# A decoder layer on one core: the four-bit quantisation of the normalised row split over two chunks of the cross-attention

## The reference, cut to what matters

```python
def fp4_quant_dequant(x):
    xb = x.reshape(shape[:-1] + (shape[-1] // BLOCK, BLOCK))      # BLOCK = 16
    scale = jnp.max(jnp.abs(xb), axis=-1, keepdims=True) / 6.0
    scale = jnp.maximum(scale, jnp.float32(1e-12))
    xn = xb / scale
    idx = jnp.searchsorted(_MID, jnp.abs(xn))
    q = _GRID[idx] * jnp.sign(xn) * scale
...
# cross-attention: q = ln(x) @ W.T + b
logits = jnp.einsum('bqd,bmd->bqm', q, memories) + add_mask
out = jnp.einsum('bqm,bmd->bqd', jax.nn.softmax(logits, axis=-1), memories)
# feed-forward
gate = fp4_linear(x, w_gate)
y = fp4_linear(x, w_up)
h = jax.nn.silu(gate) * y
return fp4_linear(h, w_down)
...
x = x + _L0_attn_ref(_layernorm(x), ...)
x = x + _L0_xattn_ref(_layernorm(x), ...)
x = x + _L0_ffn_ref(_layernorm(x), ...)
```

## Time and profile before

| what | us |
|---|---|
| median of 3 runs (lowest, highest) | 549.69 (549.15, 549.93) |
| the profiled execution | 550.32 |
| its span | 548.6 |
| around the span | 1.7 |
| TensorE busy in the span | 497.0 (91%) |
| VectorE busy | 360.2 (66%) |
| ScalarE busy | 335.9 (61%) |
| GpSimd busy | 170.9 (31%) |

### The profile page before, as it was taken

How to read it: one execution, slowest core, us unless ns; L and a number is a source line. 1 busy time by engine, 2 the same in 40 slices (tenths; PEclk the granted TensorE clock), 3 DMA queues, 4 the chain that set the end, 5 groups by cost and what they waited for, 6 DMA issues and landing times.

```text
span 548.6 us, 9765 instructions
## 1 busy us (share of the span) xinstructions
PE 497.0 (91%) x3480; PEld 324.7 (59%) x3480; DVE 360.2 (66%) x858; ACT 335.9 (61%) x659; POOL 170.9 (31%) x292
## 2 busy tenths in 40 slices
PE   7359899999999999988979989989898998989997
PEld 6206333333333333324548979979797897878896
DVE  6899988878887778813554365647666466664345
ACT  4626777787877787886663746637274472637520
POOL 6820124544444443335434231322223112210000
PEclk9857999999999999999998999989999898999999
DMA  8985300042006100030597324343243433400000
GB/s 241 289 263 119 89 1 2 4 119 57 1 3 142 35 1 4 1 118 8 161 295 219 116 87 135 87 125 109 77 116 91 117 92 82 140 25 1 6 6 6
DMA packets 27956, 49.22 MB, mean 90 GB/s; under 512 B 4140, under 2 KB 15860, under 8 KB 27332
## 3 DMA queue, kind: packets, MB, share of 16 engines
q1 hardware_dynamic: 27156, 47.87, 31.3%
q0 software_dynamic: 224, 0.54, 0.4%
q10 hardware_dynamic: 528, 0.18, 0.2%
HBM read 43.67 MB, written 4.72 MB: 88 GB/s over the span
## 4 chain that ended last, share of the span: by engine, by line
PE 71%; DVE 17%; DMA 6%; issue 2%; POOL 2%; ACT 2%; SPq 0%; DVEq 0%; POOLq 0%; ACTq 0%
PE banks L979 49%; PE banks L1088 11%; PE banks L1244 6%; DVE banks L807 6%; DMA mring<-in_mask_BxSxS_ik 3%; DVE logits L883 2%; PE banks L1099 2%; DMA operands<-query_parts 1%; POOL mring L527 1%; DMA x_sb<-in_x 1%; ACT probs L672 1%; PE banks L1151 1%; PE banks L1297 1%; DVE fa L913 1%; DMA query_parts<-operand_parts 1%
## 5 line engine op out<-in xcount | busy, mean ns | idle before, releaser
L672 ACT ACTIVATE probs<-banks 128x512 f32<-128x512 f32 x288 | 160.2, 599 | 49.1 <-PE banks L979 43.6
L807 DVE CUSTOM_DVE_ANT_0 banks<-banks,decay 128x1024 f32<-128x1024 f32 x128 | 155.1, 1244 | 31.8 <-PE banks L979 31.2
L979 PE MATMUL banks<-operands 112*128 112x512 bf16 (+4 forms) x736 | 148.5, 333 | 20.9 <-DMA operands<-query_parts 14.0
L979 PEld LDWEIGHTS banks<-operands 115*128 115x128 bf16 (+1 forms) x736 | 55.3, 98 | 126.5 <-ACT probs L672 55.1
L979 PEld LDWEIGHTS banks<-mem,pT 128*128 128x128 f32 (+1 forms) x816 | 107.7, 195 | 7.8
L979 PE MATMUL banks<-mem,pT 128*128 128x128 f32 (+1 forms) x816 | 111.4, 279 | 0.0
L693 ACT ACTIVATE pT<-banks 128x512 f32<-128x512 f32 (+1 forms) x104 | 60.4, 580 | 53.7 <-PE banks L1244 53.7
L883 DVE CUSTOM_DVE_ANT_0 logits<-banks,mring 128x512 f32<-128x512 f32 (+1 forms) x85 | 56.2, 666 | 42.9 <-PE banks L979 26.7
L535 POOL TENSOR_SCALAR_AFFINE_SELECT probs<-probs 128x128 f32<-128x128 f32 x128 | 37.1, 293 | 109.7 <-ACT probs L672 107.8
L1088 PE MATMUL banks<-probs,v_ext 128*32 128x512 f32 x512 | 68.2, 605 | 0.1
L979 PE MATMUL banks<-memT_hi,qc_hi 128*128 128x512 f32 (+1 forms) x104 | 50.8, 488 | 17.4 <-DVE cmax L883 17.4
(11 more groups left out here) (169 smaller groups left out, 509.1 us busy)
## 6 DMA issues: line engine op xcount, KB each, us to landing
mring<-in_mask_BxSxS_ik SPq DMA_DIRECT2D x39, 512.0 KB, 3.5
operands<-key_parts SPq DMA_DIRECT2D x24, 192.0 KB
operands<-query_parts SPq DMA_DIRECT2D x21, 192.0 KB
key_parts<-operand_parts SPq DMA_DIRECT2D x10, 256.0 KB, 3.4
mem<-in_ctx SPq DMA_DIRECT2D x3, 832.0 KB, 9.2
mask<-in_mask_BxSxS_ik SPq DMA_DIRECT2D x9, 256.0 KB, 2.9
pT<-in_mask_BxSxS_ik SPq DMA_DIRECT2D x9, 256.0 KB, 3.0
query_parts<-operand_parts SPq DMA_DIRECT2D x4, 384.0 KB, 5.1
```

Of the source, the lines that this page charges most:

```text
L672: act.activation(probs[:, to, :], PS[:, u % 3, :], ACT.Exp).then_inc(s_p, 1)
L807: dve.tensor_tensor_reduce(out=rows, in0=rows, in1=decay[:, off:off + S], scale=1.0, scalar=-3.0e38, op0=ALU.mult, op1=ALU.max, accum_out= ...
L979: return pe.matmul(o, a, b, start=start, stop=stop, skip_group_check=alone)
```

## The change

At `c == 1` DVE still normalises the row but runs only part 0 of `quantize`. Part 1 runs at `c == 2`. Nothing is added or taken away, and the calls on PE, ACT, POOL and SP are as before.

```diff
@@ -926,7 +926,9 @@
                     dve.wait_ge(s_f2, t + 1)
                     link(dve.tensor_scalar(xn[:, t, :], x_sb[:, t, :], mv[:, t, 0:1], rstd[:, t:t + 1],
                                            ALU.subtract, ALU.mult))
-                    quantize(xn[:, t, :], xn[:, t, :], P, D // BLOCK, s_f3)
+                    quantize(xn[:, t, :], xn[:, t, :], P, D // BLOCK, s_f3, (0,))
+                if c == 2:
+                    quantize(xn[:, t, :], xn[:, t, :], P, D // BLOCK, s_f3, (1,))
                 if c == 5:
```

## The result

| | before | after |
|---|---|---|
| median, us (lowest, highest) | 549.42 (549.08, 549.93), 4 runs | 536.22 (535.53, 537.88), 4 runs |
| ratio, 95% interval | | 0.976 (0.973 to 0.979) |
| profiled execution | 550.32 | 537.88 |
| its span | 548.6 | 536.1 |

The kernel became 13.2 us faster. The forecast was 537.1 us with a range of 534.8 to 541.8. In the changed kernel the lines after the edit have moved by two: L981, L1246 and L1286 are the L979, L1244 and L1284 of before.

The account below looks back on a forecast made before the run. The prediction took TensorE as the bound, idling for late mask-adds and then running slowly. Waits of 8.0 us plus clock of 4.9 us made 12.9 us off the profiled 550.32, giving 537.1 us for the median, range 534.8 to 541.8.

Parts of the forecast that it names:

- The bottleneck: Six passes: TensorE waits 15.1 us for mask-adds that are late in VectorE's queue behind all of `quantize`, not for the DMA.
- The mask-add of chunk 1: Pass 1: it takes L915's slot at 325.47, logits follow 0.74 us later at 326.21, 2.11 us earlier than before.
- What is handed back: Pass 1: POOL holds L916, so TensorE waits at L1284 and shortly at chunk 4's logits; 1.31 of 2.11 us stay.
- The sum of the waits: Six passes: 1.31 us in each of five and 1.39 us in pass 6, 8.0 us; bounds 7.2 and 11.9 us.
- I take 1.31 us for each: Pass 1's gain applied to five passes, with POOL's start within 0.2 us of the same place: 6.6 us.
- a loss of 0.15 us: Part 1: if POOL's operation came 0.2 us later and held another operation, each pass would lose about 0.15 us more.
- The clock: TensorE's slow stretches behind three long stalls, 1.62 us each, all vanish once the stalls are shorter: 4.9 us.
- The sum: Whole kernel: 8.0 us of waits plus 4.9 us of clock, 12.9 us gained, 537.1 us predicted.
- That VectorE's part 1 wouldn't be held: Rival: POOL holds little of part 1 because its operation arrives in another order; 533.2 us, 7%.
- That the gain would be taken back in chunks 7 and 8: Rival: VectorE's steps there or ACT's exponentials take back the gain later in the pass; 543.2 us, 7%.
- that L1286 would become the longer stall: Slower rival: `xq_ready` comes so late that this instruction, L1284 before, stalls longer than the stall removed; 552.0 us, 3%.
- That the clock would still fall in the passes: Rival: shorter stalls close together lower it in two or three passes; 540.4 or 542.0 us, 18%.

Follow-up runs that it names:

- e1_fill20: Kernel before, plus 20 useless identity transposes on TensorE in the stall ahead of chunk 3's logits, passes 1 to 5; 544.99 us, ratio 0.991.
- e2_fill6: Kernel before, plus 6 useless identity transposes on TensorE in the same old stall of passes 1 to 5; 550.75 us, ratio 1.001.
- e9_again: The changed kernel, unaltered, measured once more on another chip; 535.79 us, ratio 0.974 to the kernel before.
- e6_shift2: As e5_shift, with the normalisation and part 0 also moved from c == 1 to c == 2; 543.80 us, ratio 0.988.
- e4: Changed kernel with POOL converting only 8 of 1,024 columns of each mask piece, a measurement only; 527.54 us, ratio 0.960.
- e5_shift: Changed kernel with part 1 at c == 3 and every later feed-forward step one chunk later on PE, ACT and DVE; 550.52 us, ratio 1.000.

## Why the prediction was right, and where it was not exact

**The bottleneck.** Right. TensorE's wait for the mask-add was VectorE's queue, not the mask's DMA, although the chain of waits named the DMA. After the change the mask-add starts right behind L913, with the DMA where it was: POOL's operation behind that DMA starts at 327.50, 0.83 us after the mask-add. Were the chain true, the mask-add would have waited for it.

**The mask-add of chunk 1.** Right: from part 0's end 0.04 us, then 0.75 us to the logits (0.74 forecast). From the logits of chunk 2 to those of chunk 3 the gain is 2.10 us in pass 1, forecast 2.11.

**What is handed back.** Right in its place and nearly in size. In pass 1 the logits of chunk 4 come 5.70 us after those of chunk 2, against 7.11 before: 1.41 us stay, 1.31 were forecast. L916 is held, as assumed. One step of the forecast is off by the rows that it names: L916 was to end 0.14 us after POOL's operation, which ended at 327.52, so at 327.66 and not "near 327.53", and then 1.18 us would have stayed; 327.53 needs an operation of 1.04 us, the length that it has now. Measured, L916 ended 0.09 us after POOL's.

The mask-adds aren't held. This one stands wholly beside POOL's work in the changed kernel and takes 0.69 us, as the others do:

```profile
345.51 0.69 DVE L883 CUSTOM_DVE_ANT_0 logits<-banks,mring 128x512 f32<-128x512 f32 x1 [0.28 <-DVE cmax L883]
345.32 2.17 POOL L527 TENSOR_SCALAR mring<-mring 128x1024 f32<-128x1024 int32 x2
```

The rule of the Trainium skill, SBUF — State Buffer, section "Who interferes with whom", on the port pair that VectorE and GpSimd share and that one of them holds for a whole instruction, agrees with both rows: L916 waited for POOL's operation, and the mask-add, with one input in PSUM and one in SBUF, fits those that by that section don't contend.

**The sum of the waits was mis-sized by 10%.** The passes gained 13.65 us, of which three slow stretches at 1.62 us are 4.86; that leaves 8.8 us instead of 8.0. The step at fault is "I take 1.31 us for each". Pass 6 kept 1.38 us, as forecast (1.39), pass 1 1.41, and the other four 1.5 us each on average. There POOL's operation falls a little later against part 1, and holds L917 and not L916; L916 runs before it. This is pass 3, VectorE and POOL:

```profile
388.37 0.23 DVE L916 TENSOR_SCALAR fa<-fa 128x128 f32<-128x128 f32 x1
388.64 1.01 DVE L917 TENSOR_TENSOR fa<-fa 128x128 f32<-128x128 f32 x1
388.39 1.12 POOL L527 TENSOR_SCALAR mring<-mring 128x1024 f32<-128x1024 int32 x1 [2.09 <-DMA mring<-in_mask_BxSxS_ik]
```

More is done before the hold, so less is left behind it. I had put the difference between passes down as a loss of 0.15 us; it was a gain of about as much.

**The clock.** The size was right and e1_fill20 measures it alone: 4.9 us. The reason I gave for none being left was partly wrong, so that none was left is partly luck. I argued by the length of one stall, since falls stood only behind 2.6 to 2.7 us; e2_fill6 has three behind 2.0 to 2.1 us. And the stretch near 255 us of the changed kernel comes some 1.5 us after a stall of 1.10 us, in a part where TensorE is idle for 1.25 of 4 us (e9_again). In the kernel before the same rows stand there with the same stall of 1.11 us and a clock of 1.00. So neither one length nor the rows alone decide. What held in the six passes of all eleven profiles is weaker: every slow stretch there stands behind a stall of 2.0 us or more, and no stall of up to 1.74 us brought one; but of the stalls of 2.0 us or more, four brought none (passes 1 and 3 of the kernel before, pass 4 of e2_fill6, one of e6_shift2's). What exactly decides a fall stays open. It also varies from one execution to the next: those of the kernel before beside e1 to e4 range from 548.1 us at a mean clock of 0.966 to 553.8 us at 0.957.

**The sum.** 12.9 us forecast, 13.2 measured between the medians. That these are so close is partly chance: the passes alone gained 13.65. In the profiled executions it was 12.4: 13.65 in the passes and 0.05 behind them, less 1.2 ahead of them, and near 0 around the span. The times of the rivals start from 549.9 us, the highest of the runs and not their median of 549.69, and two of them are 0.1 us off by their own terms (540.3 and 533.1); nothing hangs on either.

**The rivals.** That VectorE's part 1 wouldn't be held is refuted by its timeline (L916 1.09 us, L917 1.01). That the gain would be taken back in chunks 7 and 8, and that L1286 would become the longer stall, are refuted by the account and the waits of the changed kernel: 13.65 us stayed, and L1286 waits 0.4 us at most. That the clock would still fall in the passes is refuted by its two profiles. The two about later stalls are real mechanisms of this kernel, though. e5_shift is the slower rival with its place moved: a quantised row that comes late under two POOL operations and lowers the clock. I gave its like 3% for this edit, and missed it in my own.

## What to carry to other kernels

Where an in-order engine serves a busy one, put what the busy engine waits for first, and cut a long helper step at the point where that becomes ready; then ask what waits for the second half, and give it a later place too. Count a stall twice: for its own length and for the slow clock behind it, which here was 4.9 of 13 us. Before moving a step by one place, look at what else runs at its new place, on the other engine that can hold its operations as well; a shift that is free at one step can cost 2.8 us a pass at another.

## What the runs showed of the hardware that I had not expected

- Filler work speeds the kernel up. Twenty useless transposes in each of five stalls of 2.6 to 2.7 us took 4.9 us off; six of them took off nothing.
- The granted clock can fall to its lower level (1.2 of 2.4 GHz) in a stretch whose longest stall is 1.1 us, and stay at 1.00 behind one of 2.68 us.
- POOL's mask conversion, 43.8 us in 46 operations that nobody waits for in the six passes, costs the changed kernel 8.7 us, nearly all of it by holding VectorE's there.
- A stall costs more than the idle time in its brackets. In pass 1 of the changed kernel the logits of chunk 3 start 1.18 us after their transposes instead of 0.36, 0.82 us lost, where the row shows 0.58 us of idleness.
